# Moving the last 60 count scatters from the third FFN's gate and route to its experts

## The reference

```
x = x + _L0_gnn_ref(_layernorm(x, axis=-1), ...)
x = x + _L0_ffn_ref(_layernorm(x, axis=-1)[None], ...)[0]
... L1_gnn, L1_ffn, L2_gnn ...
x = x + _L2_ffn_ref(_layernorm(x, axis=-1)[None], ...)[0]
x = x + _L3_gnn_ref(_layernorm(x, axis=-1), ..., edge_index)
x = x + _L3_ffn_ref(_layernorm(x, axis=-1)[None], ...)[0]
```

```
logits = jnp.einsum('bsd,de->bse', xn, Wr) + br
top_vals, top_idx = jax.lax.top_k(logits, K)          # K = 2 of E = 8
w = jax.nn.softmax(top_vals, axis=-1)
for e in range(E):
    h = jax.nn.gelu(jnp.einsum('bsd,dh->bsh', xn, W1[e]) + b1[e], approximate=False)
    y = y + (jnp.einsum('bsh,hd->bsd', h, W2[e]) + b2[e]) * w_full[..., e, None]
```

## Time and profile before

| what | value |
|---|---|
| median of 3 runs | 5015.8 us (5006.75 to 5021.97) |
| profiled execution | 5025.15 us, of which 5023.4 us lie between its first and last instruction |
| PE busy | 3385.1 us (67%) |
| POOL busy | 2043.2 us (41%) |
| DVE busy | 1969.7 us (39%) |
| mean granted clock of TensorE | 0.784 of full speed |
| count scatters (L133) | 416, 423.9 us busy on POOL, mean 1019 ns |

### The profile page before, as it was taken

How to read it: one execution, slowest core, us unless ns; L and a number is a source line. 1 busy time by engine, 2 the same in 40 slices (tenths; PEclk the granted TensorE clock), 3 DMA queues, 4 the chain that set the end, 5 groups by cost and what they waited for, 6 DMA issues and landing times. The chain is left out here.

```text
span 5023.4 us, 50647 instructions
## 1 busy us (share of the span) xinstructions
PE 3385.1 (67%) x14657; PEld 2324.6 (46%) x14657; DVE 1969.7 (39%) x5074; ACT 1211.3 (24%) x3052; POOL 2043.2 (41%) x2054
## 2 busy tenths in 40 slices
PE   3878762397888883211787783425993985798796
PEld 2666651284544442200564552212561663347686
DVE  5545565215666668500797123000005435102101
ACT  3444430032222221100785111000011212103232
POOL 4666637403555557577001542773006433000021
PEclk8676675698988886555898897656996997898798
DMA  4444420004776661200663332102413214342112
GB/s 155 160 161 155 162 101 14 0 1 146 210 200 194 185 195 57 77 10 19 197 242 132 101 99 86 61 13 72 151 59 128 64 63 142 118 153 86 38 37 74
DMA packets 278409, 542.54 MB, mean 108 GB/s; under 512 B 61218, under 2 KB 187110, under 8 KB 277508
## 3 DMA queue, kind: packets, MB, share of 16 engines
q1 hardware_dynamic: 199876, 396.17, 23.5%
q0 software_dynamic: 78272, 143.18, 10.6%
HBM read 370.70 MB, written 168.47 MB: 107 GB/s over the span
## 5 line engine op out<-in xcount | busy, mean ns | idle before, releaser
L1172 PE MATMUL bank<-layer_gnn_h_nodes,layer_gnn_s_onehot_t 128*128 x1664 | 554.3, 462 | 96.2 <-issue 58.8
L1124 POOL DMA_INDIRECT layer_gnn_s_rows<-gat_rows,src_cols x416 | 401.7, 966 | 366.9 <-DMA kept_rows<-layer_gnn_s_rows 208.1
L1421 PE MATMUL bank<-layer_gnn_w_onehot,layer_gnn_w_part 128*128 128x128 f32 x1664 | 308.8, 317 | 333.3 <-issue 247.8
L143 POOL DMA_INDIRECT edge_weights<-shares,share_cell x416 | 461.3, 1109 | 128.4 <-issue 128.4
L2522 PE MATMUL bank<-layer_gnn_b_weights,xn_nodes 128*128 128x400 f32 x768 | 319.0, 555 | 286.4 <-issue 216.7
L495 POOL DMA_INDIRECT layer_gnn_sum_rows<-xn_rows,src_cols x416 | 424.6, 1021 | 199.4 <-issue 102.2
L133 POOL DMA_INDIRECT edge_counts<-repeats,count_cell x416 | 423.9, 1019 | 126.4 <-issue 126.4
L1421 PEld LDWEIGHTS bank<-layer_gnn_w_onehot,layer_gnn_w_part 128*128 128x128 f32 x1664 | 237.8, 208 | 404.6 <-issue 269.1
L554 PE MATMUL bank<-layer_gnn_sum_onehot,layer_gnn_sum_rows 128*128 128x128 f32 x1664 | 363.9, 381 | 80.5 <-issue 55.3
L1172 PEld LDWEIGHTS bank<-layer_gnn_h_nodes,layer_gnn_s_onehot_t 128*128 128x128 f32 x1664 | 320.5, 214 | 195.0 <-issue 119.8
L554 PEld LDWEIGHTS bank<-layer_gnn_sum_onehot,layer_gnn_sum_rows 128*128 128x128 f32 x1664 | 315.2, 277 | 132.0 <-issue 89.5
(11 more groups left out here) (599 smaller groups left out, 5672.1 us busy)
## 6 DMA issues: line engine op xcount, KB each, us to landing
kept_rows<-layer_gnn_s_rows SPq DMA_DIRECT2D x104, 512.0 KB
layer_gnn_w_rows<-kept_rows SPq DMA_DIRECT2D x104, 512.0 KB
edge_weights<-layer_gnn_sum_zeros SPq DMA_DIRECT2D x56, 800.0 KB
layer_gnn_b_weights<-edge_weights SPq DMA_DIRECT2D x56, 800.0 KB
layer_gnn_gcn_sum_counts<-edge_counts SPq DMA_DIRECT2D x50, 896.0 KB
layer_gnn_s_dst_across<-in_dst_row SPq DMA_DIRECT2D x104, 256.0 KB
edge_counts<-layer_gnn_w_no_edges SPq DMA_DIRECT2D x25, 896.0 KB
layer_ffn_e_w<-in_l1f_w SPq DMA_DIRECT2D x16, 1024.0 KB
```

The costliest lines, as they stand in the source:

```text
L143: nc.gpsimd.indirect_dma_start(g.weights, bass.IndirectOffsetOnAxis(ap=g.share_cell[:, t:t + 1].bitcast(U32), axis=0), g.shares[:, t:t + 1 ...
L1124: nc.gpsimd.indirect_dma_start(rows[:, t % U, :], None, htable, bass.IndirectOffsetOnAxis(ap=g.srcc[:, t:t + 1].bitcast(U32), axis=0)).the ...
L1172: last = nc.tensor.matmul(g.ps[4 + t % 4][:, 0:D + HEADS], onehot_t[:, t % 4, k, :], hflat[:, ds(w * AW + (k * AW + HEADS), D + HEADS)], s ...
L1421: last = nc.tensor.matmul(g.ps[t % 4][:, c * P:(c + 1) * P], part[:, t % 4, c * P:(c + 1) * P], onehot[:, t % 4, :], start=True, stop=True)
```

## The change

The scatters 356 to 416 are no longer issued in the gate block and the route block. They are issued in the experts' block, two after each tile's put and take, for the tiles t = 0 to 29 (the `min` makes the rest of the calls empty). Nothing else is changed.

```diff
-COUNTED = (20, 116, 356, 386)
+COUNTED = (20, 116, 356)
...
-                      flat[:, E * (H2 + D):E * (H2 + D) + D], clear_pads(r, 2, flat[:, E * (H2 + D):E * (H2 + D) + D]), gamma, beta, g_cols, b_cols, load_experts,
-                      lambda pool: place_counts(nc, g, pool, COUNTED[2], COUNTED[3]))
-            route(nc, g, "mo_route", logits, 2, None, None, r, g.acc, table, lambda pool: place_counts(nc, g, pool, COUNTED[3], ET))
+                      flat[:, E * (H2 + D):E * (H2 + D) + D], clear_pads(r, 2, flat[:, E * (H2 + D):E * (H2 + D) + D]), gamma, beta, g_cols, b_cols, load_experts)
+            route(nc, g, "mo_route", logits, 2, None, None, r, g.acc, table)
...
                     if t + IN < T2:
                         take_rows(nc, r, table, rows[:, t % IN, :], t + IN).then_inc(loaded[t % IN], 16)
+                    place_counts(nc, g, pool, min(COUNTED[2] + 2 * t, ET), min(COUNTED[2] + 2 * t + 2, ET))
```

## The result

The changed kernel took 5056.8 us (median of 4 runs, 5050.1 to 5061.0), before took 5011.3 us beside it (4 runs). The ratio is 1.0092, 95% interval 1.0061 to 1.0124: slower by 45.5 us, where 5012 us was predicted and a change within 0.3%.

The account below looks back on a forecast made before the run. It took PE to bound the experts' block and POOL's drain the hole before it. Gate block -1.3, route -22.4 and experts +20.2 us gave -3.5 us, from the median 5015.8 to 5012 us; 8-in-10 range 4999 to 5032 us.

Parts of the forecast that it names:

- What bounds the kernel: Third FFN: PE bounds the experts' block; a 19 us hole before it waits for POOL's drain behind queued scatters.
- the route, -22.4 us: Route block: without scatters, the time from DVE's last operation to the first take falls from 23.6 to 1.2 us.
- the tail of 18.9 us: End of the route block: POOL's drain ends 18.9 us after the last scatter; counted as removed within the route's gain.
- The gate block, -1.3 us: End of the gate block: without scatters, DVE's wait of 2.78 us falls to 1.51 us, gaining 1.3 us.
- The experts, +20.2 us: Experts' block: four scatters per pair make POOL late, so PE is held 20.2 us at turns of pairs 9 to 18.
- POOL's lag: Experts' block: POOL needs 10.22 us per pair against PE's 8.20, falling behind 2.02 us per pair, 28.3 us by pair 14.
- The drain's tail was chance, or stays: Rival, route's drain: tail varies or stays, so little is gained; +13.4 us, or +22.9 with a longer experts' drain; chance 0.20.
- The clock: Rival, experts' block: TensorE's granted clock falls to 0.64 in the stalls, making the change +22.5 us (5038); chance 0.08.
- The experts lose little: Rival, experts' block: lag is hidden better, change -13.7 us, or -23.7 us with nothing lost (4992); chance 0.12.
- The rule of the Trainium skill's page: Experts' block: VectorE copies may shut GpSimd out of its descriptor port; would make the change +31 us; left out of the sum.
- the prediction's own sum: Whole kernel: gate block -1.3, route -22.4 and experts +20.2 us add up to -3.5 us.

Follow-up runs that it names:

- e5: The kernel of before, unchanged, profiled again on a chip of the slower kind: 5012.6 us.
- e9: The changed kernel, unchanged, on a chip of the faster kind: 3994.1 us against 3986.5 us for before, ratio 1.0020.
- e1: The kernel of before with the last 60 count scatters left out, on the faster kind of chip: 3955.0 us against 3984.2 us, ratio 0.9925.
- e13: The changed kernel with the last edge tile's scatter cut to its first 16 rows, on the faster kind of chip: 3979.6 us, ratio 0.9981 to before.
- e16: The kernel of e13 run once more, again on the faster kind of chip: 3976.3 us against 3986.4 us for before.
- e10: The changed kernel with the experts' 60 scatters replaced by gathers of 2-byte cells, on the faster kind of chip: 3974.1 us, experts 270.0 us.
- e7: Before with the last 60 scatters placed anew, 24 in the third graph layer's sums, 36 in the experts, one a tile; slower chip: 5032.4 us, ratio 1.0029.
- e17: The kernel of e10 run once more, on the slower kind of chip: 5052.1 us against 5018.1 us for before, ratio 1.0072.
- e4: The kernel of before with the third graph layer's 240 count scatters left out, on the faster kind of chip: 3972.5 us, ratio 0.9975.
- e6: The changed kernel, unchanged, measured again on the slower kind of chip: 5057.9 us against 5012.6 us for before, ratio 1.0092.

## Why the prediction was wrong

*What bounds the kernel; the route, -22.4 us.* Right: -23.1 us on kind A, -23.0 on B. The drain takes 0.87 us without indirect DMAs in its block. But the tail of 18.9 us, of which the prediction said "What sets it the trace doesn't tell", doesn't belong to the route. It belongs to the last edge tile, whose scatter the change moved into the experts with the others.

*The gate block, -1.3 us.* A mis-sized term: -10.6 us. The step took DVE's end at 3820.54 us for what the block needs anyway, since POOL ended within 1.5 us of it. On kind A that end was itself late, held by PE, whose matmuls and signals come late with the scatters (PE's waits by "issue" are 17.9 us in e5, 5.6 in the changed kernel on the same kind, and 5.2 on B). Two engines that end together are no proof that neither waits for the other. The second FFN's gate block was there to compare in length, not only at its end.

*The experts, +20.2 us.* The step that failed: it made POOL's lag the only cost, and PE's waits for takes the only path. On kind A, where the change was measured, the experts lost 66.5 us, and by another path: PE waited 7.8 us for takes, 5.7 of them for the first, and POOL, which was to have no idle time for 15 pairs, waited 42.9 us for DVE in them (on kind B, e9, 8.9 us, for the first put). On kind B the mechanism is there, where nothing else happens: against e1's 252.2 us the loss is +19.8 us in e13, +18.6 in e16 and +17.8 in e10. That the size comes so close is in part luck, since e13's waits are 16.7 us and 3.8 us are longer work of PE, which the sum didn't have. What the step left out is two costs of the transfers themselves:

- the last edge tile, 123 writes to one cell: 287.6 - 272.0 = 15.6 us on kind B, in the middle of the experts, where takes and puts queue behind it;
- the slowing of PE's starts and of what leaves PE when indirect transfers are added, on kind A only: +66.5 us against before's experts, where on B it is 287.6 - 251.1 = +36.5 us, so 30 us more for the same kernel.

On kind A the parts don't simply add, since an engine that PE keeps waiting gives POOL time to catch up. How much of the 66.5 us each has there isn't separated; the runs without the padding met only kind B, and so did the memsets that hold POOL without transfers. The loss without lag is shown there (e7, +25 us by tile 32) and the loss without padding (e17, 324.8 - 251.2 = +74 us for 60 reads).

The assumption behind both is that a scatter costs POOL's 0.96 us and nothing else. The trace of before could have refuted it: in the third graph layer PE starts a matmul every 2.8 us as long as scatters are issued and for 23 us more, and every 0.33 us after. I read the stages around the change and not the one other stage where the same instructions run in hundreds.

*The rivals.* "The drain's tail was chance, or stays" came nearest: the tail stayed with its tile and moved. Its mechanism, that it varies, is wrong. The clock: 0.90 from 3960 to 4060 us, where under 0.80 would have decided. It fell behind stalls, and the late signals shown above belong to matmuls that ran at the full clock. It isn't free either: between 3886 and 4064 us it stood at its lower level for 37.6 us in all, so at most half of that, some 19 of the 23.7 us of longer work, is its share by estimate. "The experts lose little" is false at full POOL time (and by its own sum it would decide at a loss under 23.7 - 15 = 8.7 us, not 8.6). The rule of the Trainium skill's page "SBUF — State Buffer", section "SBUF: two separate sides", which would have added 2.5 us a pair to POOL, doesn't decide here: scatters beside the experts' DVE operations took 0.97 to 0.98 us. But each of those operations reads a bank of matmul results, where the one beside the stretched scatter read SBUF alone. They are not of one kind, as the prediction had it, so the experts' rows didn't try the rule.

By the prediction's own sum with the terms of kind B (e9 against e4), -11.1 - 22.9 + 36.5 = +2.5 us, where e9's medians differ by +8; with those of kind A, -10.6 - 23.1 + 66.5 = +32.8 us, where the medians differ by 45. The two profiled executions differ by 35.9 us, of which 3 lie outside this FFN; the other 10 are a difference between executions, which for before alone spread over 27 us.

## What to carry to other kernels

Before moving an instruction, look at every place of the trace where many of its kind run, and ask what the *other* engines do there, not only what it costs its own: a stretch of eight times slower matmuls was in plain sight. A tail behind a queue belongs to one transfer; find which, and whether padding sends all its rows to one address, before giving the tail to the block that ends there. And indirect transfers go best where PE is idle and the block's end isn't waiting for them; where they must run beside PE, one for every tile of work rather than two keeps the issuing engine out of lag.

## What the runs showed of the hardware that was not expected

- 123 writes of one indirect DMA to one 2-byte cell of device memory take 0.15 us each, one after the other, and later transfers of POOL's queue are complete only when they are: puts and takes up to 20.5 us after their issue in place of 2.4 and 2.8. Scatters of tiles without padding are complete 2.2 us after their issue begins.
- The same program takes 5011 to 5018 us on some chips and 3984 to 3987 us on others. On the former PE starts 36 matmuls in 100 us beside 80 scatters of single cells, on the latter 299. Reads of 2-byte cells do it like writes. 112 indirect transfers of 1 KB rows in 251 us don't, but the block of 416 gathers of such rows is 80 us longer there too, so size alone doesn't decide. Blocks without indirect DMAs take the same time on both kinds to under 2 us.
- On the former, PE stays slow for 23 us after the last scatter ended (from 3451.0 to 3474 us in before), though no transfer starts after 3452 us. Why stays open. One more difference shows in the traces: the changed kernel has 16,349 records of semaphore updates by DMAs there (16,502 in e6) and 43,694 on the latter (e9), for the same instructions. The timed executions were recorded by the profiler like the others (each has its granted clock on record), so it may be the recording that holds PE up on those chips; no run without it tells.
